# State sums of an RWKV layer in 64x32 tiles of the TensorE array, with values masked four ways

## The reference

```
def step(s, inp):
    k_l, v_l, w_l, r_l = inp
    a = k_l[..., :, None] * v_l[..., None, :]            # 16x16 per head
    out = jnp.einsum('bhs,bhst->bht', r_l, faaaa * a + s)
    s_new = a + w_l[..., None] * s
    return (s_new, out)
_, outs = jax.lax.scan(step, s0, seq)                    # 256 steps
y = group_norm(outs) * gn_w + gn_b
x = x + y * g @ Wo.T                                     # then the channel mix fWk, fWr, fWv
```

## Time and profile before

| | |
|---|---|
| median of 3 runs | 839.34 us (838.2 to 840.02) |
| profiled execution, its own time | 841.52 us |
| its span in the trace | 839.7 us, so 1.8 us lie around it |
| busy, share of the span | PE 91%, DVE 71%, ACT 44%, POOL 36% |
| mean granted TensorE clock | 0.967 of full speed |

### The profile page before, as it was taken

One profiled execution on the slowest core, in us unless ns is written; L12 is line 12 of the kernel. 1 busy time (PEld: TensorE's weight loads), 2 busy tenths in 40 slices (PEclk: granted clock), 3 DMA queues, 4 the chain that ended last, 5 costly groups with the idle time before them and its releaser, 6 DMA issues. The chain is left out here.

```text
span 839.7 us, 17973 instructions
## 1 busy us (share of the span) xinstructions
PE 762.6 (91%) x7386; PEld 512.9 (61%) x7386; DVE 597.5 (71%) x1118; ACT 370.4 (44%) x733; POOL 299.8 (36%) x297
## 2 busy tenths in 40 slices
PE   8899899986999898999899899988989899899777
PEld 6568567762686456865686457745766458447343
DVE  2662796769847688868858697588866988797641
ACT  1322123751267422763258405853356346427611
POOL 2221462108511473228520762046512751460000
PEclk9999999998998998999999999999989999999979
DMA  8661241101000000001000010001000100010000
GB/s 297 200 246 35 76 162 66 52 25 53 1 26 2 26 26 27 2 2 51 27 2 1 6 47 28 1 20 32 2 2 2 51 2 2 1 52 2 27 25 25
DMA packets 17601, 36.28 MB, mean 43 GB/s; under 512 B 2416, under 2 KB 3952, under 8 KB 17520
## 3 DMA queue, kind: packets, MB, share of 16 engines
q1 hardware_dynamic: 14624, 33.30, 11.5%
q10 hardware_dynamic: 2896, 1.84, 0.7%
HBM read 26.75 MB, written 8.39 MB: 42 GB/s over the span
## 5 line engine op out<-in xcount | busy, mean ns | idle before, releaser
L2542 POOL TENSOR_TENSOR xmix<-xmix,xa 128x512 f32<-128x512 f32 x80 | 97.4, 1241 | 230.8 <-DVE xmix L1795 230.7
L2564 POOL TENSOR_TENSOR prod<-R,K 128x512 f32<-128x512 f32 x96 | 106.3, 1138 | 39.0 <-DVE R L1852 21.3
L1364 ACT ACTIVATE st<-av,half 32x512 f32<-32x512 f32 x64 | 74.5, 1164 | 9.7 <-DVE av L1922 8.2
L1795 DVE SCALAR_TENSOR_TENSOR xmix<-CHPA,chan,sx 128x256 f32<-128x256 f32 x128 | 52.9, 475 | 21.6 <-PE CHPA L511 12.5
L530 PE MATMUL PC<-sqb,sq_fWk 128*128 128x256 f32 x256 | 64.2, 405 | 4.2 <-DVE sqb L1988 4.2
L678 PE MATMUL PC<-sq_Wo,y 128*128 128x512 f32 x128 | 64.9, 652 | 1.5 <-DVE y L1958 1.5
L530 PE MATMUL PB<-xmix,sq_Wk 128*128 128x256 f32 x256 | 59.7, 384 | 4.2 <-ACT W L1263 4.2
L537 PE MATMUL PC<-sq_fWr,sxc 128*128 128x512 f32 x128 | 62.1, 628 | 0.0
L537 PE MATMUL PC<-sq_fWv,kk 128*128 128x512 f32 x128 | 59.9, 604 | 1.5 <-ACT xc L1410 1.5
L530 PE MATMUL PB<-xmix,sq_Wv 128*128 128x256 f32 x256 | 60.8, 388 | 0.3 <-ACT K L1274 0.3
L1897 DVE TENSOR_REDUCE yred<-av 128x64 f32<-128x512 f32 (+1 forms) x96 | 60.9, 674 | 0.2
(11 more groups left out here) (170 smaller groups left out, 1379.8 us busy)
## 6 DMA issues: line engine op xcount, KB each, us to landing
x<-x_rows SPq DMA_DIRECT2D x15, 512.0 KB, 3.3
x<-in_x SPq DMA_DIRECT2D x8, 512.0 KB, 5.7
x_rows<-x SPq DMA_DIRECT2D x8, 512.0 KB, 2.9
out_x<-x SPq DMA_DIRECT2D x8, 512.0 KB, 3.2
y<-in_ctx SPq DMA_DIRECT2D x7, 512.0 KB, 4.3
sq_Wv<-in_square SPq DMA_DIRECT2D x1, 1024.0 KB, 13.0
sq_Wo<-in_square SPq DMA_DIRECT2D x1, 1024.0 KB, 15.9
sq_Wk<-in_square SPq DMA_DIRECT2D x1, 1024.0 KB, 6.3
```

What stands on the lines that cost most here:

```text
L1364: act.activation(st[dst:dst + 32, :, q // 2, :, lo:lo + S], blocks, ACT.Copy, scale=half[src, 0:1]).then_inc(st_ready, 1)
L1795: i = dve.scalar_tensor_tensor(xmix[:, SLOT_OF[name], ct, :], src[:, ct * L:(ct + 1) * L], vec("maa_" + name, ct), sx[:, ct, :], ALU.add, ...
L2542: pool.tensor_tensor(m, m, xa[:, ct:ct + 2, 1:L + 1], ALU.add).then_inc(mix_ready, 1)
L2564: pool.tensor_tensor(by_pair(prod[:, ct, :], h), r, k, ALU.mult).then_inc(prod_pool, 1)
```

## The change

`b_sums` uses 64x32 tiles: 64 partitions (four blocks) at a time, 128 columns of output. For this `b_vrow` writes four masked copies of the values (block modulo 4, with the new constant `quarter`) in place of two. The copies do not lie in a buffer of their own: `K0`, `V0`, `K1`, `layer0_w` become parts of one buffer `KV` of six, and the four copies take four neighbouring parts, over the keys and values of the sequence itself, which have been transposed by then. So key and value of a later sequence now wait for `sum_mm` (sums done) where they waited for the transposes, and `SPARE_V` alternates the other way. `sum_begun` is gone: the two halves write different banks. `b_visit` goes column tile by column tile, and inside it over the row groups. All five lists have a new order.

```
-    SPARE_V = [0, 0, 1, 0, 1, 0, 1, 0]
+    SPARE_V = [0, 0, 0, 1, 0, 1, 0, 1]
-        layer0_w = sb("layer0_w", [P, F])   K1, K0, V0 = ...   vz = sb("vz", [P, TT, 2, C])
+        KV = sb("KV", [P, 6, F])            quarter = sb("quarter", [P, 4])
+        K0, V0, K1, layer0_w = (KV[:, n, :] for n in [0, 1, 4, 5])
+        VZ = [0, 1, 0, 2, 0, 2, 0, 2]
+        vz = [KV[:, n:n + 4, :].rearrange("p e (t c) -> p t e c", t=TT) for n in VZ]
     b_visit (PE):
-                for q in range(4):
-                    rows = slice(32 * q, 32 * (q + 1))
-                    for ct in range(CT):
+                for ct in range(CT):
+                    for q in range(4):
+                        rows = slice(32 * q, 32 * (q + 1))
                         o = 32 * ((q + ct) % 4)
     b_sums (PE):
-                pe.wait_ge(vrow_ready, 4 * (u + 1))
+                pe.wait_ge(vrow_ready, 8 * (u + 1))
-                for g in [0, 2, 1, 3]:
-                    if g % 2:
-                        pe.wait_ge(sum_begun, 4 * u + 2 * t + g // 2 + 1)
-                    ne = 1 if t == 1 and g == 3 else 2
-                    rows = slice(32 * g, 32 * (g + 1))
-                    for ct in range(CT):
-                        for q in range(4):
+                for ct in range(CT):
+                    for q in range(4):
+                        for g in range(2):
+                            ne = 3 if t == 1 and g == 1 else 4
+                            rows = slice(64 * g, 64 * (g + 1))
     a_key, a_value (ACT):
-                    act.wait_ge(k_turned, TT * (a - 1))
+                    act.wait_ge(sum_mm, 4 * (a - 1))
-                    act.wait_ge(v_turned, TT * (last + 1))
+                    act.wait_ge(sum_mm, 4 * (last + 1))
     b_vrow (ACT):
+                act.wait_ge(v_turned, TT * (u + 1))
                 for t in range(TT):
-                    act.wait_ge(v_turned, TT * u + t + 1)
-                    for e in range(2):
-                        act.activation(vz[:, t, e, :], ..., scale=half[:, e:e + 1])
+                    for e in range(4):
+                        act.activation(vz[u][:, t, e, :], ..., scale=quarter[:, e:e + 1])
     lists (two of some 1,400 entries; the rest of the list is moved in the same way):
-                b_reads(7, 1)
                 c_value(6, 1, 0)
```

More of the change, by code:

```diff
@@ L72, in build_xattn_rwkv @@
         half = sb("half", [P, 2])
+        quarter = sb("quarter", [P, 4])
         eps_c = sb("eps_c", [P, TT])
@@ L187, in build_xattn_rwkv @@
             sem(n) for n in ["prod_dve", "prod_pool", "chunk_mm", "av_ready", "red_ready", "yint_ready"])
-        k_turned, krow_ready, v_turned, vrow_ready, sum_begun, sum_mm = (
-            sem(n) for n in ["k_turned", "krow_ready", "v_turned", "vrow_ready", "sum_begun", "sum_mm"])
+        k_turned, krow_ready, v_turned, vrow_ready, sum_mm = (
+            sem(n) for n in ["k_turned", "krow_ready", "v_turned", "vrow_ready", "sum_mm"])
         U_first, U_half, U_ready, scanned, st_ready, st_odd, read_mm = (
@@ L624, in b_sums @@
             def b_sums(u, t):
-                pe.wait_ge(vrow_ready, 4 * (u + 1))
+                pe.wait_ge(vrow_ready, 8 * (u + 1))
                 if t:
                     pe.wait_ge(U_ready, 8 * u + 4)
-                for g in [0, 2, 1, 3]:
-                    if g % 2:
-                        pe.wait_ge(sum_begun, 4 * u + 2 * t + g // 2 + 1)
-                    ne = 1 if t == 1 and g == 3 else 2
-                    rows = slice(32 * g, 32 * (g + 1))
-                    for ct in range(CT):
-                        for q in range(4):
[L635 to L638, removed]
+                for ct in range(CT):
+                    for q in range(4):
+                        c = slice(ct * P + 32 * q, ct * P + 32 * (q + 1))
+                        for g in range(2):
+                            ne = 3 if t == 1 and g == 1 else 4
+                            rows = slice(64 * g, 64 * (g + 1))
+                            o = CH[32 * q:32 * (q + 1)].rearrange("p (n c k) -> p n c k", c=CT, k=32)[:, 4 * g:4 * g + ne, ct, :]
+                            mm = pe.matmul(o, krow[rows, t, c], vz[u][rows, t, 0:ne, c], start=True, stop=True)
+                            if ct == CT - 1 and q == 3:
+                                mm.then_inc(sum_mm, 1)
             def b_reads(u, t):
@@ L1188, in program @@
                 c_turn_y(7, 0)
+                b_reads(7, 1)
+                c_wo(7, 0, 0)
                 c_turn_y(7, 1)
-                c_wo(7, 0, 0)
                 c_wo(7, 0, 1)
@@ L1331, in b_vrow @@
             def b_vrow(u):
-                act.wait_ge(w_const, 32)
+                act.wait_ge(w_const, 48)
                 if u:
                     act.wait_ge(sum_mm, 4 * u)
+                act.wait_ge(v_turned, TT * (u + 1))
                 for t in range(TT):
-                    act.wait_ge(v_turned, TT * u + t + 1)
-                    for e in range(2):
-                        act.activation(vz[:, t, e, :], CH[:, t * C:(t + 1) * C], ACT.Copy,
-                                       scale=half[:, e:e + 1]).then_inc(vrow_ready, 1)
+                    for e in range(4):
+                        act.activation(vz[u][:, t, e, :], CH[:, t * C:(t + 1) * C], ACT.Copy,
+                                       scale=quarter[:, e:e + 1]).then_inc(vrow_ready, 1)
             def b_first(u):
```

806 lines of the change are left out of this document (402 added, 404 removed).

## The result

The changed kernel takes **790.12 us** (median of 4 runs, 789.49 to 790.49), the kernel before 839.68 in the same session (838.2 to 840.89): ratio 0.941, 95% interval 0.9393 to 0.9427. That is 49.5 us less. The forecast was 832, the range 823 to 844: the sign is right, the size is not.

The account below looks back on a forecast made before the run. PE's list, busy 91% of the span, was taken as the bound. Terms -10.0 + 0 + 3.6 - 2.5 + 1.7 = -7.2 us gave 834.3 from the profiled 841.5, or 832 us on the median of 839.3; range 823 to 844.

Parts of the forecast that it names:

- sums, 64x32: In b_sums on PE: eight tiles run at a time, so busy time falls from 27.6 to 17.6 us, -10.0 us.
- visits, inner order: In b_visit on PE: either order issues the same 16 tiles and ends at the same time, 0 us.
- value copies, new lists: In b_vrow on ACT: 32 more copies, partly covered by PE's new list before the sums, net +3.6 us.
- order, all of it: New order of the lists: -2.5 us at the first visits and +1.7 us at the end.
- visits of sequence 1: Waits for POOL's products filled by decay steps between visits 0 and 1 and c_wo parts between 2 and 3: -2.1 - 2.2 us.
- the end: Second half's reads come behind the first half's transpose, so its half of c_wo ends later: +1.7 us.
- rival D: Filled waits also spare PE half-speed stretches, three of 2 us, and sums cost 0.89 us a call: 824 us, chance 0.18.
- A: In the sums, the two row halves of a column don't run together: +1.9 instead of -10.0, 844 us, chance 0.10.
- B: The gain is given back in the chain from transposes through copies, sums, scan and states to reads: 838.5 us, chance 0.17.
- C: In the visits, row tiles on one PSUM bank run one after the other: about +95 us, 935, chance 0.02.
- The two waits: At the sums of sequences 0 and 2, PE waits for ACT's value copies: 0.9 and 1.0 us missing cover.

Follow-up runs that it names:

- e14: Kernel before with all five new lists and 32x32 sums, each value copy done twice: 799.14 us, ratio 0.9523.
- e3: Changed kernel with the visits' inner order put back to row group by row group: 790.35 us, ratio 0.9396.
- e1: Kernel before with the five new lists and nothing else of the change: 797.19 us, ratio 0.9473.
- e7: Kernel before with the new lists only from the end of visit 0 to key part 3 of sequence 1's visits: 835.19 us, ratio 0.9959.
- e12: Changed kernel with the old order of its end (second reads of sequence 7, ACT's and DVE's steps) put back: 789.59 us, ratio 0.9408.
- e2: Changed functions (64x32 sums, four masked copies, new visit order) with the old lists, one piece of sequence 1 moved: 854.84 us, ratio 1.0141.
- e13: Kernel before with each value copy done twice, 32x32 sums and old lists: 871.83 us, ratio 1.0393.
- e5: Kernel before with extra matmuls nobody reads in PE's waits in sequences 1, 2 and the last: 833.83 us, ratio 0.992.
- e9: e2 with one of PE's own calls moved ahead of b_sums(u, 0) in seven sequences: 852.25 us, ratio 1.0155.

## Why the prediction was wrong

Its terms against what the runs showed:

| term | predicted | measured |
|---|---|---|
| sums, 64x32 | -10.0 | -9.0 (e14 to changed), -9.3 busy |
| visits, inner order | 0 | 0 (e3) |
| value copies, new lists | +3.6 | +2.0 (e14; 4 by ratio) |
| order, all of it | -0.8 (-2.5 and +1.7) | **-42.5** (e1) |
| of it: visits of sequence 1 | -4.3 | -3.4 (e7) |
| of it: the end | +1.7 | 0 (e12) |

Without the order the sum was -6.4, and going from e1 to the changed kernel gives -7.1 (-5.3 by the ratios): the new tiles themselves were priced rightly. **The step that failed is the term of the order**: I priced the three places at which I had compared the lists and took all the rest of PE's 77.1 us of idle time as standing. The calls of the other periods had been moved just as much, and each piece is worth something: 10.8 us in the period of sequence 1, where I had 4.3, and 10.8 us of lead already at visit 0 of sequence 1, where I had nothing. "Sequences 2 and 3 have 0.8 and 1.8 us less work between the reads and visit 1" counted work in one gap; a list is better when the waits of all engines fit, and that the reading of a few rows doesn't give. The same fault is in the term of the copies: I added up what the new list puts between transposes and sums, and never what the old one had there. It had half as much (20.3 against 42.7 us), which would have shown how far the lists differ outside the three places.

The second fault is that the slow clock was left out of the sum and came in only as rival D, with three stretches of 2 us. The rows for it were there: a mean clock of 0.967 is 55 us at half speed, 27 us of work, of which the change gave back 16.7. D had the right direction, but at 824 it still lies 34 us above what was measured.

Of the rivals: A is out (seven tiles begun where there were four, 1.09 us a call), C too (e3). B, the gain given back in a chain through the copies, is wrong for the changed kernel but is what the tiles do in the old lists: e2, with e13 for the copies. The prediction said what would break it, PE's idle time changing by more than 5 us; it fell by 24.8.

The two waits that I expected at the copies' end in sequences 0 and 2 are 0 and 0.39 us, in 6 there is none, and in 7 it is 1.39, not 2: eight copies back to back take 4.74 us, not 8 x 0.697 = 5.6, since neighbours overlap. The rows had it: 32 copies of 697 ns were busy for 19.4 us, four for 2.42.

What stays open: which single moves in the lists carry the 42.5 us. The engines' lists could be exchanged only in whole stretches for all engines together, since they wait for one another in their order, so no run tells PE's part from ACT's, DVE's and POOL's. Open too is how much of it the order as such earned. The two stands on "issue" ahead of sums (3.7 us, with 13.6 us at half speed beginning at them, so up to 10.5 us) are gone in e1, but also in e5, e2 and e9, which keep the old lists or nearly so.

## What to carry to other kernels

When hand-written lists change throughout, don't price the places you have looked at and leave the rest: take the whole idle time of the bounding engine and its whole time at half speed as what is at stake, and make the range that wide. An edit has no price by itself: 32 copies cost 2 us in one order and 32 in another. And when you price cover for a longer producer, count what the old list has there as well as the new one. Useless matmuls in a wait can pay: six in the last 40 us took 3.2 us off. In the middle of the kernel part of it came back in the waits behind, and no run here separates the rest from other causes.

## What the runs showed of the hardware

- The granted clock can fall to half during a short wait in a busy stretch, but a wait of that length does not always bring it. Before, PE's timeline and the windows around 616 us (sums of sequence 5), and a window around another wait:

```profile
612.22 1.65 PE L637 MATMUL CHPA<-vz,prod 32*32 32x64 f32 x127 [0.31 <-DVE av L1915]
615.92 0.21 PE L637 MATMUL CHPA<-vz,prod 32*32 32x32 f32 x1 [2.05 <-issue]
616.05 3.78 PE L537 MATMUL PC<-sq_fWr,sxc 128*128 128x512 f32 x4
```

```profile
608.00:612.00 4.00, 3.91 (x93) 1.00 0.01 2
612.00:616.00 4.00, 1.73 (x128) 0.87 0.02 4
616.00:620.00 4.00, 4.00 (x6) 0.50 0.00 0
```

```profile
560.00:580.00 20.00, 14.71 (x149) 1.00 0.16 53
```

  PE stands still for 2.05 us, and the four records behind it take 3.78 us, where four of this size take 1.88 at full speed (`a_theta`). Between 560 and 580 us PE waits 2.07 us for POOL, and the visit behind it takes 0.73 us, at full clock throughout. So the length of a wait alone does not tell. What held the last record of the call is not shown: it is one of the two places of "issue" in the earlier trace rows. The trace has one packet of the DMA queue of instructions beginning 0.7 us before each of the two (at 613.2 and 252.1 us); most of the 58 such packets are followed by no stand, so a cause is not shown. In e13 14.5 us more of waits came with 33 us more at half speed, in e2 21.4 us more with none.
- In 0.08 us PE begins seven records of 128 columns in 64x32 tiles, and four of 64 columns in 32x32 ones; a call takes 1.09 us against 1.66.
